# Operands of TensorE moved to multiples of 2048 bytes, and squares of 1024 columns taken in halves

## What is computed

```python
y = einsum('bct,bcd->bdt', x, cond_weights[index])   # 128 x 64 x 1024
z = einsum('bsd,od->bso', y, W) + b                  # W 1024 x 1024
u = einsum('bsd,edr->ebsr', y, A)                    # 8 experts of rank 16: 128 columns
m = einsum('ebsr,ero,e->bso', u, B, p_scores)
gamma = minimum(0.5 * norm(z) / (norm(m) + 1e-6), 1.0)   # norms over the 1024 columns
out = x + z + gamma * m
```

## Time and profile before

| | |
|---|---|
| median of 3 runs | 952.65 us (952.53 to 954.38) |
| the profiled execution | 954.46 us, span of the trace 952.6 us |
| TensorE (matmul) busy | 918.7 us, 96% of the span |
| TensorE (weight load) busy | 789.8 us, 83% |
| VectorE busy | 583.6 us, 61% |
| ScalarE busy | 357.7 us, 38% |
| GpSimd busy | 346.1 us, 36% |
| DMA engines | 75.17 MB, mean 79 GB/s |

### The profile page before, as it was taken

One profiled execution on the slowest core, in us unless ns is written; L12 is line 12 of the kernel. 1 busy time (PEld: TensorE's weight loads), 2 busy tenths in 40 slices (PEclk: granted clock), 3 DMA queues, 4 the chain that ended last, 5 costly groups with the idle time before them and its releaser, 6 DMA issues. The chain is left out here.

```text
span 952.6 us, 15191 instructions
## 1 busy us (share of the span) xinstructions
PE 918.7 (96%) x4876; PEld 789.8 (83%) x4876; DVE 583.6 (61%) x903; ACT 357.7 (38%) x704; POOL 346.1 (36%) x336
## 2 busy tenths in 40 slices
PE   6589999999999999999999999999999999999995
PEld 4478888888888888888888888888888888888883
DVE  4995566665556565556565556666555656555653
ACT  4353343434333434334334334343433343432431
POOL 2623344332244433234433234433224443323442
PEclk8699999999999999999999999999999999999998
DMA  8201222211222221122121122221122222112201
GB/s 260 78 23 69 92 92 69 91 65 48 91 91 76 84 87 47 70 91 91 69 91 45 67 91 91 69 91 67 48 88 91 81 79 90 45 69 91 92 23 66
DMA packets 32457, 75.17 MB, mean 79 GB/s; under 512 B 12729, under 2 KB 13754, under 8 KB 32442
## 3 DMA queue, kind: packets, MB, share of 16 engines
q1 hardware_dynamic: 32442, 74.99, 22.4%
HBM read 41.42 MB, written 33.55 MB: 79 GB/s over the span
## 5 line engine op out<-in xcount | busy, mean ns | idle before, releaser
L400 ACT CAST y_hi<-mix_ps 128x512 fp32r<-128x512 f32 x128 | 75.7, 591 | 322.9 <-PE mix_ps L739 322.9
L331 POOL TENSOR_TENSOR stats<-stats 128x1 f32<-128x1 f32 x32 | 17.7, 554 | 447.1 <-ACT squares L447 447.1
L575 DVE TENSOR_TENSOR s_lo<-s,s_hi 128x512 fp32r<-128x512 f32 x128 | 142.1, 1129 | 4.9 <-ACT s_hi L413 0.6
L317 POOL TENSOR_TENSOR z<-z,x_in 128x512 f32<-128x512 f32 x64 | 82.7, 1293 | 130.4 <-ACT squares L428 130.4
L739 PEld LDWEIGHTS mix_ps<-mixer,x_in 128*128 128x128 f32 x1024 | 124.0, 191 | 5.9 <-issue 1.0
L739 PE MATMUL mix_ps<-mixer,x_in 128*128 128x128 f32 x1024 | 124.6, 275 | 0.5 <-DMA mixer<-in_L_cond_weights_dram 0.5
L413 ACT CAST s_hi<-s 128x512 fp32r<-128x512 f32 x128 | 79.0, 618 | 114.3 <-POOL s L305 96.5
L554 DVE TENSOR_TENSOR y_lo<-mix_ps,y_hi 128x512 fp32r<-128x512 f32 x128 | 87.9, 687 | 53.9 <-ACT s L406 48.6
L752 PE MATMUL b_ps<-w_hi,y_hi 128*128 128x512 f32 x256 | 102.1, 399 | 7.9 <-DVE z L640 4.8
L752 PE MATMUL b_ps<-w_hi,s_hi 128*128 128x512 f32 x256 | 100.5, 392 | 9.4 <-DVE w_lo L535 9.4
L752 PE MATMUL c_ps<-w_hi,s_hi 128*128 128x512 f32 x256 | 102.4, 400 | 1.9 <-issue 1.8
(11 more groups left out here) (92 smaller groups left out, 1835.7 us busy)
## 6 DMA issues: line engine op xcount, KB each, us to landing
x_in<-in_x_dram SPq DMA_DIRECT2D x64, 512.0 KB, 3.6
out_dram<-z SPq DMA_DIRECT2D x64, 512.0 KB, 2.7
w_lo_raw<-in_L_ffn_W_dram SPq DMA_DIRECT2D x12, 256.0 KB, 7.2
mixer<-in_L_cond_weights_dram SPq DMA_DIRECT2D x128, 16.0 KB, 2.1
w_hi_raw<-in_L_ffn_W_dram SPq DMA_DIRECT2D x4, 256.0 KB, 3.7
bias<-in_L_ffn_b_dram SPq DMA_DIRECT2D x1, 512.0 KB, 5.0
a_lo_raw<-in_L_ffn_A_dram SPq DMA_DIRECT2D x1, 512.0 KB, 7.3
b_lo_raw<-in_L_ffn_B_dram SPq DMA_DIRECT2D x1, 512.0 KB, 7.9
```

Source lines behind the costliest of these rows:

```text
L317: nc.gpsimd.tensor_tensor(z0[:, par, cols], z0[:, par, cols], x_in[:, 2 * par, cols], ALU.add).then_inc(residual0_ready, 1)
L331: nc.gpsimd.tensor_tensor(stat(NORM_Z, 1), stat(Z_SQ, 1), half, ALU.pow).then_inc(norm_z_ready[1], 1)
L400: nc.scalar.copy(y_part(y_hi, r, h), mixed(h)).then_inc(y_hi_ready, 1)
L575: nc.vector.tensor_tensor(s_lo[:, n, :, :], s_raw(n), s_hi[:, n, :, :].bitcast(fp32), ALU.subtract).then_inc(s_lo_ready, 1)
```

## The change

All large tensors are declared in another order. The small `mixer`, `cond_ids` and `stats` come first and take 1664 bytes from 16,512 on; then `w_hi` (and the raw loads that lie in the same place) is aligned to 2048 bytes and begins at 18,432. By the declared sizes, `w_lo`, `a_lo`, `b_lo`, `a_hi`, `b_hi`, `x_in`, `y_hi`, `y_lo`, `s_hi`, `s_lo` and `u_hi` then begin at multiples of 2048 too, and `u_lo` at a multiple of 1024. `mixer` stays at 16,512. The scratch tile `squares` shrinks from 1024 to 512 columns of bf16, or there would be no room. So three squares of a pair (z1, m1, m0) are taken in two halves, each with its own sum, each waiting for the half before it since they write the same scratch; GpSimd adds the two sums before it takes the root. The semaphores `z1_squared` and `m_squared` now count two for each pair.

```diff
--- before.py
+++ after.py
@@ -60,8 +60,8 @@
     ctx = ExitStack()
     with ctx:
-        def sb(name, shape, dt):
-            return ctx.enter_context(nc.sbuf_tensor(name, shape, dt))
+        def sb(name, shape, dt, align=32):
+            return ctx.enter_context(nc.sbuf_tensor(name, shape, dt, align_bytes=align))
         def pb(name, shape):
             return ctx.enter_context(nc.psum_tensor(name, shape, fp32))
@@ -70,48 +70,55 @@
             return ctx.enter_context(nc.semaphore(name))
+        mixer = sb("mixer", [P, 2, P], fp32)
+        cond_ids = sb("cond_ids", [1, B], i32)
+        stats = sb("stats", [P, 32], fp32)
         with ExitStack() as loaded:
-            w_hi_raw, w_lo_raw = (loaded.enter_context(nc.sbuf_tensor(name, [P, 7, HC, H], fp32))
+            w_hi_raw, w_lo_raw = (loaded.enter_context(nc.sbuf_tensor(name, [P, 7, HC, H], fp32, align_bytes=2048))
                                   for name in ("w_hi_raw", "w_lo_raw"))
             a_lo_raw = loaded.enter_context(nc.sbuf_tensor("a_lo_raw", [P, KC, XR], fp32))
             b_lo_raw = loaded.enter_context(nc.sbuf_tensor("b_lo_raw", [P, D], fp32))
-        w_hi = sb("w_hi", [P, 7, HC, H], fp32r)
+        w_hi = sb("w_hi", [P, 7, HC, H], fp32r, 2048)
         w_lo = sb("w_lo", [P, 7, HC, H], fp32r)
         a_lo = sb("a_lo", [P, KC, XR], fp32r)
         b_lo = sb("b_lo", [P, D], fp32r)
         a_hi = sb("a_hi", [P, KC, XR], fp32r)
         b_hi = sb("b_hi", [P, D], fp32r)
-        bias = sb("bias", [P, 3, H], fp32)
-        mixer = sb("mixer", [P, 2, P], fp32)
         x_in = sb("x_in", [P, 4, D], fp32)
         y_hi = sb("y_hi", [P, KC, 2 * P], fp32r)
         y_lo = sb("y_lo", [P, KC, 2 * P], fp32r)
         s_hi = sb("s_hi", [P, 4, HC, P], fp32r)
         s_lo = sb("s_lo", [P, 4, HC, P], fp32r)
+        u_hi = sb("u_hi", [P, 2 * P], fp32r)
+        u_lo = sb("u_lo", [P, 2 * P], fp32r)
+        bias = sb("bias", [P, 3, H], fp32)
         s14 = sb("s14", [P, 2, HC, P], fp32)
         s23 = sb("s23", [P, 2, HC, P], fp32)
-        u_hi = sb("u_hi", [P, 2 * P], fp32r)
-        u_lo = sb("u_lo", [P, 2 * P], fp32r)
         z0 = sb("z0", [P, 2, D], fp32)
         z1 = sb("z1", [P, D], fp32)
-        squares = sb("squares", [P, D], bf16)
-        cond_ids = sb("cond_ids", [1, B], i32)
-        stats = sb("stats", [P, 24], fp32)
+        squares = sb("squares", [P, H], bf16)
         half = stats[:, 0:1]
         p_col = stats[:, 1:2]
         table_out = stats[:, 2:3]
-        z11_sq, z12_sq = stats[:, 3:4], stats[:, 4:5]
+        def z_sq(r, h):
+            return stats[:, 3 + 2 * r + h:4 + 2 * r + h]
+        def m_sq(r, h):
+            return stats[:, 7 + 2 * r + h:8 + 2 * r + h]
         def stat(n, r):
-            return stats[:, 6 + 2 * n + r:7 + 2 * n + r]
-        Z_SQ, M_SQ, NORM_Z, NORM_M, TWICE_M, HALF_OVER_M, GAMMA = range(7)
+            return stats[:, 11 + 2 * n + r:12 + 2 * n + r]
+        Z_SUM, M_SUM, NORM_Z, NORM_M, TWICE_M, HALF_OVER_M, GAMMA = range(7)
         lo, up_ = slice(0, H), slice(H, D)
-        idle = squares[:, lo]
+        idle = squares[:, :]
         raw11 = w_hi_raw[:, T4, :, :]
         raw21 = w_lo_raw[:, T4, :, :]
         raw12 = w_lo_raw[:, T3, :, :]
@@ -180,7 +187,8 @@
         z12_squared = sem("z12_squared")
         z1_squared = sem("z1_squared")
         m_squared = [sem(f"m{r}_squared") for r in range(2)]
-        z0_sum_ready = sem("z0_sum_ready")
+        z_sum_ready = [sem(f"z{r}_sum_ready") for r in range(2)]
+        m_sum_ready = [sem(f"m{r}_sum_ready") for r in range(2)]
         norm_z_ready = [sem(f"norm_z{r}_ready") for r in range(2)]
         norm_m_ready = [sem(f"norm_m{r}_ready") for r in range(2)]
         residual0_ready = sem("residual0_ready")
@@ -307,7 +315,7 @@
             def residual1(p, slot):
-                pool.wait_ge(z1_squared, p + 1)
+                pool.wait_ge(z1_squared, 2 * p + 2)
                 nc.gpsimd.tensor_tensor(z1[:, :], z1[:, :], x_in[:, slot, :], ALU.add).then_inc(residual1_ready, 1)
             def residual0(p, par, h):
@@ -321,21 +329,25 @@
                 pool.wait_ge(z11_squared, p + 1)
                 pool.wait_ge(z12_squared, p + 1)
-                nc.gpsimd.tensor_tensor(stat(Z_SQ, 0), z11_sq, z12_sq, ALU.add).then_inc(z0_sum_ready, 1)
-                pool.wait_ge(z0_sum_ready, p + 1)
-                nc.gpsimd.tensor_tensor(stat(NORM_Z, 0), stat(Z_SQ, 0), half, ALU.pow).then_inc(norm_z_ready[0], 1)
+                nc.gpsimd.tensor_tensor(stat(Z_SUM, 0), z_sq(0, 0), z_sq(0, 1), ALU.add).then_inc(z_sum_ready[0], 1)
+                pool.wait_ge(z_sum_ready[0], p + 1)
+                nc.gpsimd.tensor_tensor(stat(NORM_Z, 0), stat(Z_SUM, 0), half, ALU.pow).then_inc(norm_z_ready[0], 1)
             def norm_z1(p):
-                pool.wait_ge(z1_squared, p + 1)
-                nc.gpsimd.tensor_tensor(stat(NORM_Z, 1), stat(Z_SQ, 1), half, ALU.pow).then_inc(norm_z_ready[1], 1)
+                pool.wait_ge(z1_squared, 2 * p + 2)
+                nc.gpsimd.tensor_tensor(stat(Z_SUM, 1), z_sq(1, 0), z_sq(1, 1), ALU.add).then_inc(z_sum_ready[1], 1)
+                pool.wait_ge(z_sum_ready[1], p + 1)
+                nc.gpsimd.tensor_tensor(stat(NORM_Z, 1), stat(Z_SUM, 1), half, ALU.pow).then_inc(norm_z_ready[1], 1)
             def norm_m(p, r):
-                pool.wait_ge(m_squared[r], p + 1)
-                nc.gpsimd.tensor_tensor(stat(NORM_M, r), stat(M_SQ, r), half, ALU.pow).then_inc(norm_m_ready[r], 1)
-            nc.gpsimd.memset(squares[:, :], 0.0).then_inc(idle_set, 1)
+                pool.wait_ge(m_squared[r], 2 * p + 2)
+                nc.gpsimd.tensor_tensor(stat(M_SUM, r), m_sq(r, 0), m_sq(r, 1), ALU.add).then_inc(m_sum_ready[r], 1)
+                pool.wait_ge(m_sum_ready[r], p + 1)
+                nc.gpsimd.tensor_tensor(stat(NORM_M, r), stat(M_SUM, r), half, ALU.pow).then_inc(norm_m_ready[r], 1)
+            nc.gpsimd.memset(idle, 0.0).then_inc(idle_set, 1)
             nc.gpsimd.memset(mixer[:, :, :], 0.0).then_inc(mixer_zeroed, 1)
             nc.gpsimd.memset(half, 0.5).then_inc(half_set, 1)
             pool.wait_ge(half_set, 1)
@@ -424,49 +436,58 @@
                 act.wait_ge(z11_ready, p + 1)
                 if not opening:
                     act.wait_ge(z12_squared, p)
-                    act.wait_ge(z0_sum_ready, p)
-                nc.scalar.activation(squares[:, lo], z0[:, par, lo], ACT.Square,
-                                     accum_out=z11_sq).then_inc(z11_squared, 1)
+                    act.wait_ge(z_sum_ready[0], p)
+                nc.scalar.activation(squares[:, :], z0[:, par, lo], ACT.Square,
+                                     accum_out=z_sq(0, 0)).then_inc(z11_squared, 1)
             def square_z12(p, par, before):
                 act.wait_ge(z12_ready, p + 1)
-                act.wait_ge(before, p + 1)
-                nc.scalar.activation(squares[:, lo], z0[:, par, up_], ACT.Square,
-                                     accum_out=z12_sq).then_inc(z12_squared, 1)
+                act.wait_ge(before, 2 * p + 2)
+                nc.scalar.activation(squares[:, :], z0[:, par, up_], ACT.Square,
+                                     accum_out=z_sq(0, 1)).then_inc(z12_squared, 1)
             def square_z1(p, opening):
-                act.wait_ge(z21_ready, p + 1)
-                act.wait_ge(z22_ready, p + 1)
-                if opening:
-                    act.wait_ge(z11_squared, 1)
-                else:
-                    act.wait_ge(m_squared[0], p)
-                    act.wait_ge(norm_z_ready[1], p)
-                nc.scalar.activation(squares[:, :], z1[:, :], ACT.Square,
-                                     accum_out=stat(Z_SQ, 1)).then_inc(z1_squared, 1)
+                for h in range(2):
+                    act.wait_ge(z22_ready if h else z21_ready, p + 1)
+                    if h:
+                        act.wait_ge(z1_squared, 2 * p + 1)
+                    elif opening:
+                        act.wait_ge(z11_squared, 1)
+                    else:
+                        act.wait_ge(m_squared[0], 2 * p)
+                        act.wait_ge(z_sum_ready[1], p)
+                    nc.scalar.activation(squares[:, :], z1[:, h * H:(h + 1) * H], ACT.Square,
+                                         accum_out=z_sq(1, h)).then_inc(z1_squared, 1)
             def square_m1(p, opening):
                 act.wait_ge(m_done[1], p + 1)
-                act.wait_ge(z1_squared, p + 1)
                 if not opening:
-                    act.wait_ge(norm_m_ready[1], p)
-                nc.scalar.activation(squares[:, :], m_ps[:, :], ACT.Square,
-                                     accum_out=stat(M_SQ, 1)).then_inc(m_squared[1], 1)
+                    act.wait_ge(m_sum_ready[1], p)
+                for h in range(2):
+                    if h:
+                        act.wait_ge(m_squared[1], 2 * p + 1)
+                    else:
```

(20 more changed lines are left out.)

## The result

| | before | changed |
|---|---|---|
| median of 20 runs | 953.88 us (952.53 to 956.40) | 956.81 us (955.07 to 957.45) |
| ratio | 1 | 1.0026, 95% interval 1.0018 to 1.0033 |
| span of the profiled execution | 952.6 us | 954.9 us |
| ScalarE busy | 357.7 us | 379.8 us |
| GpSimd busy | 346.1 us | 375.2 us |

The ratio is not the quotient of the two medians, which would be 1.0031; the means, 954.03 and 956.49 us, lie 2.5 us apart. One execution of the kernel before, taken beside the experiments, lasted 1887.21 us, twice as long as all others (952.5 to 956.6), and is in no ratio.

A forecast was written before the change was run, and what follows sets the result against it. TensorE, busy all 500 us from 400 to 900, was taken as the bound. Alignment 0, pair 1 +0.9 and the end +0.3 on the median of 952.65 gave 953.9 us; own range 951.5 to 957, stretched to 907 to 960.

The forecast's parts named there:

- Alignment brings 0 of 49.6 us: TensorE's fp32r matmuls at full clock: aligned operands likelier gain 0 us; removing all 13.3 ns of excess would gain 49.6 us.
- a fixed start-up of the fp32r path: TensorE: an explanation of the 13.3 ns excess per fp32r matmul that fits the rows as well as a misaligned start.
- Rival B: TensorE: alignment removes the fp32r excess, part given back in waits before W21; 907 to 926 us, taken 915; chance 0.25.
- The halves and sums, +0.91 to +1.37 us on the way to `p1_biased`: Chain before W21: 0.37 for z1's halves, 0.27 for each of two sums, up to 0.46 more on GpSimd.
- The meeting of `residual1` and the S2 split: Loop: GpSimd's later residual1 overlaps VectorE's split_s(S2); the small GpSimd operation behind takes +0.46 us, as in pair 1.
- rival C: Loop: same pace, but the added chain outgrows its 1.55 us cover and W21 waits; 958.4 to 962 us; chance 0.14.
- Hidden in 30 pairs, 0.2 to 0.6 us left: Loop: the delay before W21 stays under the 1.55 us of room, so TensorE does not wait in 30 pairs.
- Pair 1, +0.9 us: Pair 1 has no room, so TensorE's wait before W21 grows by 0.9 us (0.9 to 1.4), from 1.35 to 2.3.
- The end, +0.3 us: Last pair: squares finish as before, and only one added sum of 0.27 us stands on the chain.
- "Same": Sign of the whole change: no difference beyond about 0.2% (1.9 us); chance 0.45.
- "slower": Sign of the whole change: slower by more than about 0.2% (1.9 us); chance 0.28.

The follow-up runs named there:

- experiment 1: The changed kernel with the old declaration order and no alignment, halved squares and added sums kept: 956.31 us, ratio 1.0032 to the kernel before.
- experiment 2: The kernel before with a pad of 32 bytes ahead of the large tensors, so operands start 160 or 1184 bytes past 2048: 954.24 us, ratio 1.0010.
- experiment 3: The kernel before, in the loop W11 in bf16 on spread high halves and T4 with 64 stationary columns: 0.225 and 0.230 us a matmul; no total time given.
- experiment 4: Old addresses, halved squares; three loop products in bf16: both operands contiguous, moving spread, stationary spread: 0.215, 0.226, 0.215 us a matmul; no total time given.
- experiment 7: The changed kernel with the sum of m1 made three times in a row in every pair: 968.44 us, ratio 1.0156 to the kernel before.

## Why the prediction was right, point by point

- **Alignment brings 0 of 49.6 us.** Right, with the reason half right. The rows had shown that crossings cost nothing; the result and experiments 1 and 2 close the case for the start. I had offered "a fixed start-up of the fp32r path". Fixed it is, the same for 256 and for 512 columns; but experiments 3 and 4 show that bf16 pays most of it too when its moving operand is spread over the same bytes. Rival B falls. The Trainium skill's lines of 16 bytes ("SBUF — State Buffer", "Door 1: The DMA port swizzle") gave the same answer; none of these runs shows such lines. The Trainium skill's spacing of 215.7 ns ("TensorE: Matmul & The Clock Gate", "Wait — 56ns, not 53.3ns?") holds for contiguous bf16 (0.215 us), not for a moving operand of four bytes a column in bf16 (0.225 to 0.226) or fp32r (0.2267).
- **The halves and sums, +0.91 to +1.37 us on the way to `p1_biased`.** Right: L661 ends at 412.46 + 0.68 = 413.14 and W21 starts at 413.53, 0.39 us later where 1.60 were, a delay of 1.21. The meeting of `residual1` and the S2 split came as the pair 1 rows said. The small operation behind it, now an addition, took 0.64 us instead of 0.19, +0.45 where I had taken +0.46; only the split got off lighter, with 1.08 us instead of pair 1's 1.80. The root after it (L348) kept its 0.55, so that not both small operations suffered, as rival C had it:

```profile
406.88 2.41 POOL L319 TENSOR_TENSOR z<-z,x_in 128x1024 f32<-128x1024 f32 x1
409.24 0.64 POOL L346 TENSOR_TENSOR stats<-stats 128x1 f32<-128x1 f32 x1
409.96 0.55 POOL L348 TENSOR_TENSOR stats<-stats 128x1 f32<-128x1 f32 x1
...
408.75 1.08 DVE L596 TENSOR_TENSOR s_lo<-s,s_hi 128x512 fp32r<-128x512 f32 x1
...
412.46 0.68 DVE L661 TENSOR_TENSOR z<-b_ps,bias 128x512 f32<-128x512 f32 x1
```

- **Hidden in 30 pairs, 0.2 to 0.6 us left.** Right: 28.26 us a pair (W21 at 413.53 and at 441.79), 0.34 left. Rival C didn't come, and experiment 7 shows its threshold where it was put. Its price was too low: 0.34 us for a shortfall of 0.20.
- **Pair 1, +0.9 us.** Right for the wait itself: 2.29 us against 1.35.
- **The end, +0.3 us.** 0.2 in the trace.
- **The size.** +1.2 us forecast, +2.9 us between the medians and +2.5 between the means; the forecast of 953.9 us was made on a median of three runs, 952.65, that itself rose to 953.88 with 20. So of the 2.9 us between 953.9 and the measured 956.81, 1.2 are the base. The measured time lies at the edge of the forecast's own range (951.5 to 957); that it lies inside 907 to 960 says little, since that range was stretched to hold rival B. The step that was mis-sized is "it grows by 0.9": I priced a longer idle stretch of TensorE at its length. The wait itself measured +0.94. It is also followed, in some executions, by a stretch of half clock, 1.4 us in the profiled one, and this term I had put at nothing: I had allowed for changes of the clock at the start only. "Same" was my likeliest sign and "slower" came.

## What to carry to other kernels

An excess over the columns that is the same for every instruction need not come from where the operands lie; before moving addresses for it, read whether operands that already start at different places differ in pace. A step put on a covered path was free here only in the steady loop: look for the one pair where the cover is not there yet, and price its wait with what an idle TensorE loses afterwards, in pace (0.10 to 0.15 us a wait here) and in clock (0 to 2.5 us). The cheap remedy was to move one instruction of the chain that TensorE waits for ahead of the ones that it doesn't.

## What the runs showed of the hardware that was not expected

- At full clock a matmul of 512 columns steps at 0.2267 us in fp32r and at 0.225 to 0.226 in bf16 with a moving operand spread over the same four bytes a column; with a contiguous bf16 one at 0.215 us. A spread stationary operand cost nothing in bf16 (0.215 us), and half as many stationary columns gained nothing in fp32r (0.230 us). The fp32 mix doesn't show this excess (5 ns over 256 columns).
- Operands that start 0, 128 or 160 bytes past a multiple of 2048 gave one pace.
- At full clock the first matmul after a wait was 0.33 to 0.35 us ahead of the next instead of 0.23, and the product behind it took 0.10 to 0.15 us longer in all, after waits of 0.20, 1.35 and 2.29 us.
- Behind a wait of 2.3 us or more, four of six traces show half clock for 3 to 6 us; behind one of 1.35 us, none of three.
- Runs of one kernel differ by up to 4 us (952.5 to 956.4 for the kernel before). Stretches of half clock that fall differently in the first 60 us, where TensorE waits for weights, account for part of it: the product S4 x W22 of pair 0 starts anywhere from 54.49 to 56.45 us in the three traces that have the changed kernel's order of work. Effects under 2 us were told from the traces, stretch by stretch, and hardly from the medians.
